# Score vectors as extra columns of the layer matrices, bias rows added inside the linear attention, and kept rows and result moved tile by tile

## The chip, the core and the metric

The kernel runs on one core of one Trainium2 chip. The metric is the device time of one execution in microseconds (us). The engines named below are TensorE (PE, with its weight loads as PEld), VectorE (DVE), ScalarE (ACT), GpSimd (POOL) and SyncE (SP, which here only issues transfers and waits).

## What is computed

Two layers of a graph transformer over 3125 nodes with 256 features. What matters here is the second layer's front and end, and the four graph attention projections. For the graph attention layers g0 (layer 0), g1, g2, g3 (layer 1), the projection is

```python
h = (x @ W).reshape(n, heads, out_ch)
al_s = jnp.einsum('nhc,hc->nh', h, a_src)      # one score per node and head
al_d = jnp.einsum('nhc,hc->nh', h, a_dst)
...
out = softmax over incoming edges(al_s[src] + al_d[dst]) applied to h[src];  return out + b
```

g0 has 4 heads of 64 features and 256 inputs, g1 4 heads of 128 and 256 inputs, g2 4 heads of 128 and 512 inputs, g3 one head of 256 and 512 inputs. Layer 1 begins with a linear attention whose output, plus a bias `b_out`, is added to X; the three graph attentions follow, then a small MLP (M1, M2, M3 with last bias `mb3`) whose output is added to the same X, and a gated feed-forward network whose output is added to X and is the result.

## The kernel before, in words

Rows are cut into T = 25 tiles of R = 125 rows; loops take U = 5 tiles an iteration. X lives in SBUF as [125, 25, 256]. The program is a row of stages (`Stage`): each has its own buffers and semaphores, and ends with a barrier of all engines. Within a stage the engines run freely against semaphores. `tile_dma` (L63) cuts each transfer into two, partitions 0 to 111 (L65) and 112 to 124 (L66). `wait_apart` is a wait followed by an increment of a tick semaphore.

**The projection stage** `stage_gat_project` (L686, stages g0p, g1p, g2p, g3p). SP loads the matrix `w`, the two score vectors `att` (broadcast to all partitions) and the bias `bt`. DVE folds each 128-row chunk of W with the score vectors into `wa` (L780, L782), so that the scores are x @ wa. Then for each tile PE makes h into the PSUM tile `psh` (L751) and the 2 x heads scores into `psa` (L753); DVE adds the bias and writes HX (L791) and writes the negated scores to AL (L794). An f32 matmul shows as two records in the trace; KC is 2 (g0, g1) or 4 (g2, g3) chunks. In g0p and g1p POOL copies the tile's columns of XT to `xs`; in g2p and g3p the rows come from DRAM by SP into five buffers, PE turns them (L742) and ACT copies them to `xs` (L804). PE may run two tiles ahead of DVE: it waits for `h_free` and `al_free` of the tile two before.

**Around the linear attention.** `stage_linear_attention` (stage lina, then linb) makes a 256 x 256 matrix WEFF. Stage lo (`stage_rows_add`) adds XT @ WEFF to X tile by tile: POOL copies, PE multiplies (L672), DVE adds (L2093). Stage ar1 (`stage_add_row`) adds two bias rows to all of X on DVE. Stage sv (`stage_move_rows`) writes X to DRAM (`kept_rows`), because the graph attentions need the SBUF space. Then g1p follows.

**Around the third graph attention.** After g1, g2 and g3, stage ld1 reads `kept_rows` back into X, stage tn (`stage_turn`) reads g3's output rows and transposes them, and the MLP and gates follow. In the attention stages (g3a) SP loads one tile row of `lowered` (`nl`, 1.5 MB) for each tile of rows.

**The end.** `stage_last_ffn` adds five products per tile to X on DVE (L2183, L2186); stage st writes X to the output in one transfer (two parts).

Of the kernel before, what the change touches and what calls it, by code (L numbers as in the profile page):

```python
# [685 lines left out]
def stage_gat_project(nc, m, g, feed, KC, w, att_s, att_d, bias, AL, HX):  # L686

    H, F, HF = g.heads, g.feat, g.heads * g.feat
    from_rows = feed.shape[0] == N
    with Stage(nc, g.name + "p") as s:  # L690
        wt = s.sb("w", [P, KC, HF])
        att, prod = s.sb("att", [P, 2, HF]), s.sb("prod", [P, 2, HF])
        wa = s.sb("wa", [P, KC, 2 * H])
# [38 lines left out]
        def _(pe):  # L732
# [23 lines left out]
            pe.wait_ge(loaded, 64)  # L756
# [1623 lines left out]
```

## Time and profile before

| | value |
|---|---|
| median of 3 runs | 5582.71 us (5581.7 to 5585.99) |
| the profiled execution | 5571.72 us, its span 5570.1 us |
| PE busy | 4657.3 us, 84% of the span |
| DVE busy | 3214.9 us, 58% |
| ACT busy | 2853.6 us, 51% |
| POOL busy | 1528.0 us, 27% |
| mean granted TensorE clock | 0.897 of full |
| moved by DMA | 479.79 MB, mean 86 GB/s |

The shares are averages over several dozen stages. What a change in one stage is worth must be read from that stage's own stretch: which engine is waited for there, and in the stretches in which nothing but a transfer runs, how long that transfer lasts.

### The profile page before, as it was taken

How to read it: one execution, taken by the hardware profiler on the slowest of the kernel's cores; microseconds unless marked ns; L12 is line 12 of the kernel's file. 1: busy time of each engine (PE TensorE's matmuls, PEld its weight loads, DVE VectorE, ACT ScalarE, POOL GpSimd, SP SyncE). 2: the span in 40 equal slices, each digit the busy share in tenths (PEclk: the TensorE clock that was granted, in tenths of full speed). 3: DMA queues.
4: the chain of work that ended last, by engine and by line, in shares of the span. 5: the costliest groups of instructions: out<-in, count | busy, mean ns of one | idle time of the engine just before them, and what ended most of it. 6: DMA issues, size and time to landing. Idle time of an engine off the chain costs nothing. (4 is left out here: it accounts for less than half of the span.)

```text
span 5570.1 us, 94226 instructions
## 1 busy us (share of the span) xinstructions
PE 4657.3 (84%) x34254; PEld 4166.0 (75%) x34254; DVE 3214.9 (58%) x2815; ACT 2853.6 (51%) x3886; POOL 1528.0 (27%) x1308
## 2 busy tenths in 40 slices
PE   1554779999998469938699999979999998897698
PEld 1453457999998369934399999948999997786454
DVE  4894213887887401134388888717888882552222
ACT  0662133777776024313078877716778773443222
POOL 3001000221222310040146666602666661010100
PEclk9776788999999589969899999989999999998767
DMA  2672011333332245520144434323443442553000
GB/s 47 110 141 39 3 69 45 91 95 87 101 92 57 84 154 182 185 81 16 47 105 102 107 98 105 82 62 94 106 103 98 108 101 58 141 129 79 7 11 23
DMA packets 212766, 479.79 MB, mean 86 GB/s; under 512 B 117787, under 2 KB 158886, under 8 KB 189417
## 3 DMA queue, kind: packets, MB, share of 16 engines
q1 hardware_dynamic: 178982, 436.39, 30.1%
q0 software_dynamic: 24720, 30.26, 2.6%
q10 hardware_dynamic: 8736, 8.39, 0.5%
q8 instruction: 252, 4.13, 0.3%
q14 instruction: 76, 0.62, 0.0%
HBM read 391.43 MB, written 83.35 MB: 85 GB/s over the span
## 5 line engine op out<-in xcount | busy, mean ns | idle before, releaser
L1105 PE MATMUL g2a_pso<-HX,g2a_wt 125*125 125x129 f32 x5000 | 602.7, 274 | 8.0 <-DVEq L952 4.7
L1105 PE MATMUL g1a_pso<-HX,g1a_wt 125*125 125x129 f32 x5000 | 603.1, 274 | 4.5 <-ACT g1a_wt L989 3.3
L1105 PE MATMUL g0a_pso<-HX,g0a_wt 125*125 125x65 f32 x5000 | 595.1, 274 | 4.8 <-ACT g0a_wt L989 3.3
L1105 PEld LDWEIGHTS g0a_pso<-HX,g0a_wt 125*125 125x125 f32 x5000 | 585.2, 193 | 5.3 <-ACT g0a_wt L989 3.4
L1105 PEld LDWEIGHTS g2a_pso<-HX,g2a_wt 125*125 125x125 f32 x5000 | 576.3, 189 | 8.4 <-DVEq L952 4.9
L1105 PEld LDWEIGHTS g1a_pso<-HX,g1a_wt 125*125 125x125 f32 x5000 | 576.8, 189 | 5.0 <-ACT g1a_wt L989 3.5
L989 ACT ACTIVATE g0a_wt<-g0a_pst 125x1000 f32<-125x1000 f32 (+1 forms) x300 | 312.0, 1040 | 199.6 <-PE g0a_pst L1092 199.6
L922 DVE SCALAR_TENSOR_TENSOR g0a_x<-g0a_als,g0a_cd,HX 125x3125 f32<-125x3125 f32 x100 | 347.4, 3474 | 110.9 <-PE g0a_pst L1092 101.7
L922 DVE SCALAR_TENSOR_TENSOR g2a_x<-g2a_als,g2a_cd,g2a_as 125x3125 f32<-125x3125 f32 x100 | 358.7, 3587 | 81.3 <-PE g2a_pst L1092 71.3
L922 DVE SCALAR_TENSOR_TENSOR g1a_x<-g1a_als,g1a_cd,g1a_as 125x3125 f32<-125x3125 f32 x100 | 358.1, 3581 | 81.4 <-PE g1a_pst L1092 71.5
L989 ACT ACTIVATE g2a_wt<-g2a_pst 125x1000 f32<-125x1000 f32 (+1 forms) x300 | 312.2, 1041 | 170.3 <-PE g2a_pst L1092 170.3
L989 ACT ACTIVATE g1a_wt<-g1a_pst 125x1000 f32<-125x1000 f32 (+1 forms) x300 | 312.2, 1041 | 169.5 <-PE g1a_pst L1092 169.5
L927 DVE CUSTOM_DVE_ANT_0 g2a_x<-g2a_x,g2a_nl 125x3125 f32<-125x3125 f32 x100 | 344.7, 3447 | 20.0 <-issue 14.3
L927 DVE CUSTOM_DVE_ANT_0 g1a_x<-g1a_x,g1a_nl 125x3125 f32<-125x3125 f32 x100 | 344.8, 3448 | 19.6 <-issue 13.9
L927 DVE CUSTOM_DVE_ANT_0 g0a_x<-g0a_x,g0a_nl 125x3125 f32<-125x3125 f32 x100 | 341.5, 3415 | 19.6 <-issue 13.9
L1092 PE MATMUL g0a_pst<-C,g0a_x 125*125 125x125 f32 x2500 | 347.1, 284 | 3.6 <-ACT g0a_x L981 3.6
L981 ACT ACTIVATE g2a_x<-g2a_x,g2a_top 125x1000 f32<-125x1000 f32 (+1 forms) x300 | 346.6, 1156 | 3.8 <-DVEq L929 3.8
L981 ACT ACTIVATE g0a_x<-g0a_x,g0a_top 125x1000 f32<-125x1000 f32 (+1 forms) x300 | 346.6, 1156 | 1.9 <-DVEq L929 1.9
L981 ACT ACTIVATE g1a_x<-g1a_x,g1a_top 125x1000 f32<-125x1000 f32 (+1 forms) x300 | 346.6, 1156 | 1.6 <-DVEq L929 1.6
L1092 PE MATMUL g1a_pst<-C,g1a_x 125*125 125x125 f32 x2500 | 322.9, 273 | 3.6 <-ACT g1a_x L981 3.6
L1092 PE MATMUL g2a_pst<-C,g2a_x 125*125 125x125 f32 x2500 | 323.0, 273 | 2.2 <-ACT g2a_x L981 2.2
L1092 PEld LDWEIGHTS g0a_pst<-C,g0a_x 125*125 125x125 f32 x2500 | 306.5, 194 | 3.8 <-ACT g0a_x L981 3.8
(428 smaller groups left out, 8429.4 us busy)
## 6 DMA issues: line engine op xcount, KB each, us to landing
g0a_nl<-lowered SPq DMA_DIRECT2D x50, 1367.2 KB
g1a_nl<-lowered SPq DMA_DIRECT2D x50, 1367.2 KB
g2a_nl<-lowered SPq DMA_DIRECT2D x50, 1367.2 KB
moe_wa<-in_L_ffn_W SPq DMA_DIRECT2D x56, 1024.0 KB, 4.9
lowered<-counts_nl SPq DMA_DIRECT2D x25, 1367.2 KB
g3a_nl<-lowered SPq DMA_DIRECT2D x25, 1367.2 KB
g0a_nl<-lowered SPq DMA_DIRECT2D x50, 158.7 KB
g1a_nl<-lowered SPq DMA_DIRECT2D x50, 158.7 KB
```

The source lines that it names most:

```text
L922: nc.vector.scalar_tensor_tensor(out=x[:, b, :], in0=als[:, h, :], scalar=cd[:, h:h + 1, ds(t, 1)].rearrange("p a b -> p (a b)"), in1=as2[ ...
L927: nc.vector.tensor_tensor_reduce(out=x[:, b, :], in0=x[:, b, :], in1=nl[:, (q + k // HG) % 2, :], scale=1.0, scalar=3e38, op0=ALU.add, op1 ...
L981: nc.scalar.activation(x[:, b, c0:c1], x[:, b, c0:c1], ACT.Exp, bias=top[:, b:b + 1], scale=-1.0).then_inc(exped, 1)
L989: nc.scalar.activation(wt[:, side, 0:n * R].rearrange("p (b n) -> p b n", b=banks), pst[0:R, 3 * side:3 * side + banks, 0:per * R], ACT.Co ...
L1092: last = nc.tensor.transpose(pst[0:R, 3 * side + j // per, col:col + R], x[:, ring(q, k), (a0 + j) * R:(a0 + j + 1) * R], m.ident[0:R, 0:R])
L1105: last = nc.tensor.matmul(pso[0:R, unit(q, 0, k) % 2, 0:F + 1], wt[:, side, j * R:(j + 1) * R], HX[:, a, q * HG + k % HG, :], start=(a == ...
```

## The change

**Projection.** Each matrix is stored in SBUF with the score vectors' products as extra columns behind it: `wt` is [P, KC, PARTS, WP + SC], where PARTS is 2 for the 512-wide layers (g1, g2) and 1 otherwise. DVE's fold writes straight into those columns. PE's matmuls make 264 (g0), 260 (g1, g2, in two halves, one PSUM bank each) or 258 (g3) columns, and the separate score matmuls are gone. DVE's two instructions a tile stay, and read the same banks. W is loaded by KC transfers, not one.

**Bias rows.** They are loaded in the linear attention stage and added to X there, one tile after each tile's `scale`; stage ar1 is gone.

**Kept rows.** Stage lo's SP stores each tile as soon as DVE has added it, and stage sv is gone; the end of g1p waits for the stores. The reload is issued by g3p's SP after its last row tile, stage ld1 is gone, and the end of stage tn waits for it.

**Result.** In the last stage DVE signals each finished tile and SP stores it; stage st is gone.

```diff
-def stage_gat_project(nc, m, g, feed, KC, w, att_s, att_d, bias, AL, HX):
+def stage_gat_project(nc, m, g, feed, KC, w, att_s, att_d, bias, AL, HX, kept=None, ahead=None):
 
     H, F, HF = g.heads, g.feat, g.heads * g.feat
+    PARTS = max(HF // 256, 1)
+    HP, WP = H // PARTS, HF // PARTS
+    SC = 2 * H // PARTS
     from_rows = feed.shape[0] == N
     with Stage(nc, g.name + "p") as s:
-        wt = s.sb("w", [P, KC, HF])
+        if kept is not None:
+            s.sems.append(kept)
+        wt = s.sb("w", [P, KC, PARTS, WP + SC])
         att, prod = s.sb("att", [P, 2, HF]), s.sb("prod", [P, 2, HF])
-        wa = s.sb("wa", [P, KC, 2 * H])
         bt = s.sb("bt", [R, HF])
         xs = s.sb("xs", [P, U, KC, R])
-        psh, psa = s.ps("psh", 3), s.ps("psa", 3)
+        ps = s.ps("ps", 3 * PARTS)
...
-            sp.dma_start(wt[:], w.rearrange("(c p) n -> p c n", p=P)).then_inc(loaded, 16)
+            for c in range(KC):
+                sp.dma_start(wt[:, c, :, 0:WP], w[c * P:(c + 1) * P].rearrange("p (x n) -> p x n", x=PARTS)).then_inc(loaded, 16)
...
+            if ahead is not None:
+                tile_dma(sp, *ahead)
+            if kept is not None:
+                sp.wait_ge(kept, 32 * T)
...
-                for c in range(KC):
-                    nc.tensor.matmul(psh[0:R, RING3[k], 0:HF], xs[:, k, c, :], wt[:, c, :], start=(c == 0), stop=(c == KC - 1))
-                for c in range(KC):
-                    last = nc.tensor.matmul(scores(k), xs[:, k, c, :], wa[:, c, :], start=(c == 0), stop=(c == KC - 1))
+                for x in range(PARTS):
+                    for c in range(KC):
+                        last = nc.tensor.matmul(banks(k)[:, x, 0:WP + SC], xs[:, k, c, :], wt[:, c, x, :], start=(c == 0), stop=(c == KC - 1))
                 last.then_inc(full, 1)
...
-                last = nc.vector.tensor_reduce(wa[:, c, :], prod[:].rearrange("p j (h f) -> p (j h) f", h=H), AX_X, ALU.add)
+                last = nc.vector.tensor_reduce(wt[:, c, :, WP:WP + SC], prod[:].rearrange("p j (h f) -> p (j h) f", h=H), AX_X, ALU.add)
...
-                    nc.vector.tensor_tensor(HX[:, ds(t, 1), :, 0:F].rearrange("p o h f -> p (o h) f"),
-                                            psh[0:R, RING3[k], 0:HF].rearrange("p (h f) -> p h f", h=H),
-                                            bt[:].rearrange("p (h f) -> p h f", h=H), ALU.add).then_inc(h_free, 1)
-                    nc.vector.tensor_scalar(AL[:, 0:2 * H, ds(t, 1)], scores(k).unsqueeze(2), -1.0, None, ALU.mult).then_inc(al_free, 1)
+                    nc.vector.tensor_tensor(HX[:, ds(t, 1), :, 0:F].rearrange("p o (x h) f -> p (o x) h f", x=PARTS),
+                                            banks(k)[:, :, 0:WP].rearrange("p x (h f) -> p x h f", h=HP),
+                                            bt[:].rearrange("p (x h f) -> p x h f", x=PARTS, h=HP), ALU.add).then_inc(h_free, 1)
+                    nc.vector.tensor_scalar(AL[:, 0:2 * H, ds(t, 1)].rearrange("p (x n) o -> p x (n o)", x=PARTS), banks(k)[:, :, WP:WP + SC],
+                                            -1.0, None, ALU.mult).then_inc(al_free, 1)
...
+                for j, v in enumerate(vectors):
+                    sp.dma_start(rows[:, j, :], v.partition_broadcast(R)).then_inc(rows_in, 16)
...
                 variance(0)
+                dve.wait_ge(rows_in, 32)
+                nc.vector.tensor_tensor(rows[:, 0, :], rows[:, 0, :], rows[:, 1, :], ALU.add)
                 for t in range(T):
                     if t + 1 < T:
                         variance(t + 1)
                     scale(t)
+                    nc.vector.tensor_tensor(X[:, t, :], X[:, t, :], rows[:, 0, :], ALU.add)
...
+            if KEEP is not None:
+                with sp.Fori(0, T // U) as i:
+                    for k in range(U):
+                        t = i * U + k
+                        wait_apart(sp, s.tick, rp.free[0], t + 3)
+                        tile_dma(sp, KEEP[:, ds(t, 1)].rearrange("p o d -> p (o d)"), cols(X[:, ds(t, 1), :]), kept)
...
+            with sp.Fori(0, T // U) as j:
+                for k in range(U):
+                    t = j * U + k
+                    wait_apart(sp, s.tick, rows_done, t + 1)
+                    tile_dma(sp, OUT[ds(t * R, R)], cols(X[:, ds(t, 1), :]), stored)
+            sp.wait_ge(stored, 32 * T)
...
+                    nc.vector.drain().then_inc(rows_done, 1)
...
-                stage_linear_attention(nc, m, a, XT, WEFF)
-                stage_rows_add(nc, m, "lo", [(XT, 2, WEFF)], X)
-                stage_add_row(nc, "ar1", [a["L1_gnn_mb3"], a["L1_mix_b_out"]], X)
-                stage_move_rows(nc, "sv", m.XS, X)
-                stage_gat_project(nc, m, g1, XT, 2, a["L1_gnn_W1"], a["L1_gnn_a_src1"], a["L1_gnn_a_dst1"], a["L1_gnn_b1"], AL, rows_of(g1))
-        for g, n in ((g1, 1), (g2, 2), (g3, 3)):
-            if n > 1:
-                stage_gat_project(nc, m, g, m.Y, 4, a[f"L1_gnn_W{n}"], a[f"L1_gnn_a_src{n}"], a[f"L1_gnn_a_dst{n}"], a[f"L1_gnn_b{n}"], AL, rows_of(g))
-            graph_attention(nc, m, g, AL, rows_of(g), m.Y[:, 0:g.heads * g.feat])
-
-
+                stage_linear_attention(nc, m, a, XT, WEFF, [a["L1_gnn_mb3"], a["L1_mix_b_out"]], X)
+                kept = nc.alloc_semaphore("rows_kept")
+                stage_rows_add(nc, m, "lo", [(XT, 2, WEFF)], X, m.XS, kept)
+                stage_gat_project(nc, m, g1, XT, 2, a["L1_gnn_W1"], a["L1_gnn_a_src1"], a["L1_gnn_a_dst1"], a["L1_gnn_b1"], AL, rows_of(g1), kept)
...
-            stage_move_rows(nc, "ld1", X, m.XS)
+            x_back = nc.alloc_semaphore("x_back")
+            stage_gat_project(nc, m, g3, m.Y, 4, a["L1_gnn_W3"], a["L1_gnn_a_src3"], a["L1_gnn_a_dst3"], a["L1_gnn_b3"], AL, rows_of(g3), None, (X, m.XS, x_back))
...
-            stage_last_ffn(nc, m, a, XT, GATE, X)
-            stage_move_rows(nc, "st", out.rearrange("(t p) d -> p t d", p=R), X)
+            stage_last_ffn(nc, m, a, XT, GATE, X, out)
```

What PE runs in two tiles of g2p before (a row with x4 is four matmuls, L742 the transposes, psh the product, psa the scores):

```order
L751 MATMUL g2p_psh<-g2p_w,g2p_xs 125x512 x4
L753 MATMUL g2p_psa<-g2p_wa,g2p_xs 125x8 x4
L742 MATMUL g2p_pst<-C,g2p_rows 128x125 x4
L747 REGISTER_ALU
L751 MATMUL g2p_psh<-g2p_w,g2p_xs 125x512 x4
L753 MATMUL g2p_psa<-g2p_wa,g2p_xs 125x8 x4
```

And the same place of the changed kernel:

```order
L761 MATMUL g2p_ps<-g2p_w,g2p_xs 125x260 x8
L751 MATMUL g2p_pst<-C,g2p_rows 128x125 x4
L756 REGISTER_ALU
L761 MATMUL g2p_ps<-g2p_w,g2p_xs 125x260 x8
L751 MATMUL g2p_pst<-C,g2p_rows 128x125 x4
```

Four wide and four narrow matmuls have become eight of 260 columns. The next piece is SP's program between the linear attention and the projection g1p, before: two stages of their own for the bias rows and the kept rows.

```order
L1189 DMA ar_v<-in_L_gnn_mb 125x256
L1189 DMA ar_v<-in_L_mix_b_out 125x256
L57 UNCONDITIONAL_BRANCH
L2203 UNCONDITIONAL_BRANCH
L65 DMA kept_rows<-X 112x6400
L66 DMA kept_rows<-X 13x6400
L57 UNCONDITIONAL_BRANCH
L707 UNCONDITIONAL_BRANCH
L709 DMA g1p_w<-in_L_gnn_W 128x2x512
```

After the change, the end of the loop in stage lo (the last of its five tiles) and what follows it:

```order
L71 REGISTER_ALU
L65 ISA
L65 DMA kept_rows<-X 112x256
L66 ISA
L66 DMA kept_rows<-X 13x256
L2099 REGISTER_ALU
L2099 COMPARE_AND_BRANCH
L57 UNCONDITIONAL_BRANCH
L711 UNCONDITIONAL_BRANCH
L714 DMA g1p_w<-in_L_gnn_W 128x2x256 x2
```

Two transfers have become fifty, issued in the loop of stage lo, and the branch to g1p stands right behind that loop. The third place is the end of g3p on SP in the changed kernel, where the reload now stands ahead of the attention's first `nl` tiles:

```order
L65 DMA g3p_rows<-attended 112x512
L66 ISA
L66 DMA g3p_rows<-attended 13x512
L721 REGISTER_ALU
L721 COMPARE_AND_BRANCH
L65 DMA X<-kept_rows 112x6400
L66 DMA X<-kept_rows 13x6400
L57 UNCONDITIONAL_BRANCH
L909 UNCONDITIONAL_BRANCH
L65 DMA g3a_nl<-lowered 112x3125
L66 DMA g3a_nl<-lowered 13x3125
```

Before, those two reload rows stood behind the whole attention stage, ahead of `tn_rows`.

## Rows read from the trace of the kernel before

**Rows 1.** Busy time by stretch: stage lo, stage sv. us, PE, PEld, DVE, ACT, POOL, PEclk, DMA share, GB/s

```profile
2650.00:2674.00 24.00, 22.72 (x100) 16.51 (x98) 10.54 (x25) 0.00 (x0) 8.90 (x23) 1.00 0.00 0
2692.60:2706.10 13.50, 0.00 (x0) 0.00 (x0) 0.00 (x0) 0.00 (x0) 0.00 (x0) 0.50 0.73 237
```

**Rows 2.** Timeline, g3p: start, us, engine, line, out<-in, count, idle before and releaser

```profile
4670.06 1.59 PEld L751 LDWEIGHTS g3p_psh<-g3p_w,g3p_xs 128*125 128x125 f32 x8
4670.16 1.89 PE L751 MATMUL g3p_psh<-g3p_w,g3p_xs 128*125 128x256 f32 x8
...
4671.89 0.93 PE L753 MATMUL g3p_psa<-g3p_wa,g3p_xs 128*125 128x2 f32 x8
...
4672.68 0.62 PE L742 MATMUL g3p_pst<-C,g3p_rows 125*128 125x125 f32 x4
...
4673.14 0.38 PE L751 MATMUL g3p_psh<-g3p_w,g3p_xs 128*125 128x256 f32 x1
```

**Rows 3.** Timeline, g2p, PE in one tile

```profile
3669.01 3.60 PE L751 MATMUL g2p_psh<-g2p_w,g2p_xs 128*125 128x512 f32 x8
...
3672.44 0.94 PE L753 MATMUL g2p_psa<-g2p_wa,g2p_xs 128*125 128x8 f32 x8
```

**Rows 4.** Timeline, g1p, PE at the start of two tiles

```profile
2725.61 1.96 PE L751 MATMUL g1p_psh<-g1p_w,g1p_xs 128*125 128x512 f32 x4
...
2727.77 0.67 PE L751 MATMUL g1p_psh<-g1p_w,g1p_xs 128*125 128x512 f32 x1
```

**Rows 5.** Timeline, g0p, PE at two tiles, DVE at one

```profile
492.72 1.11 PE L751 MATMUL g0p_psh<-g0p_w,g0p_xs 128*125 128x256 f32 x4
...
494.02 1.11 PE L751 MATMUL g0p_psh<-g0p_w,g0p_xs 128*125 128x256 f32 x4
...
494.41 0.42 DVE L791 TENSOR_TENSOR HX<-g0p_psh,g0p_bt 125x256 f32 x1 [0.79 <-PE g0p_psa L753]
...
494.75 0.16 DVE L794 TENSOR_SCALAR AL<-g0p_psa 125x8 f32 x1
```

**Rows 6.** Timeline, stage lo, DVE two tiles apart

```profile
2663.76 0.42 DVE L2093 TENSOR_TENSOR X<-X,lo_ps 125x256 f32 x1 [0.53 <-PE lo_ps L672]
...
2665.58 0.42 DVE L2093 TENSOR_TENSOR X<-X,lo_ps 125x256 f32 x1 [0.54 <-PE lo_ps L672]
```

**Rows 7.** Timeline, stage tn, SP's issues for two tiles

```profile
5131.65 0.33 SPq L65 DMA_DIRECT2D tn_rows<-attended  x1
...
5132.84 0.32 SPq L65 DMA_DIRECT2D tn_rows<-attended  x1
```

**Rows 8.** Timeline, first add of lo, first issues of ar1 and g1p

```profile
2650.98 0.42 DVE L2093 TENSOR_TENSOR X<-X,lo_ps 125x256 f32 x1 [19.21 <-PE lo_ps L672]
...
2674.00 0.33 SPq L1189 DMA_DIRECT2D ar_v<-in_L_gnn_mb  x1
...
2706.12 0.40 SPq L709 DMA_DIRECT2D g1p_w<-in_L_gnn_W  x1
```

**Rows 9.** Timeline, stage lina, DVE at the start of a tile

```profile
2621.62 1.22 DVE L1987 TENSOR_REDUCE lina_var<-lina_sq 125x16 f32<-125x1024 f32 x1 [1.99 <-ACT lina_sq L2015]
```

**Rows 10.** Timeline, end of g3a, starts of ld1 and tn

```profile
5106.03 0.52 POOL L66 DMA_DIRECT2D attended<-g3a_y  x1
5109.35 0.31 SPq L65 DMA_DIRECT2D X<-kept_rows  x1
...
5127.14 0.32 SPq L65 DMA_DIRECT2D tn_rows<-attended  x1
```

**Rows 11.** Timeline, start of g3a: first nl issue, first use

```profile
4739.54 0.33 SPq L65 DMA_DIRECT2D g3a_nl<-lowered  x1
...
4751.40 3.42 DVE L927 CUSTOM_DVE_ANT_0 g3a_x<-g3a_x,g3a_nl 125x3125 f32<-125x3125 f32 x1 [0.24 <-issue]
```

**Rows 12.** Timeline, last add of the program and the result's store

```profile
5553.57 0.48 DVE L2186 SCALAR_TENSOR_TENSOR X<-ffn_psy,GATE,X 125x256 f32 x1 [0.38 <-PE ffn_psy L2157]
5555.43 0.35 SPq L65 DMA_DIRECT2D out<-X  x1
```

More of the change, by code:

```diff
@@ L702, in stage_gat_project, with banks @@
         block = s.block()
-        def scores(k):
-            return psa[0:R, RING3[k], 0:2 * H]
+        def banks(k):
+            return ps[0:R, RING3[k] * PARTS:(RING3[k] + 1) * PARTS, :]
         @block.sync
         def _(sp):
-            sp.dma_start(wt[:], w.rearrange("(c p) n -> p c n", p=P)).then_inc(loaded, 16)
+            for c in range(KC):
+                sp.dma_start(wt[:, c, :, 0:WP], w[c * P:(c + 1) * P].rearrange("p (x n) -> p x n", x=PARTS)).then_inc(loaded, 16)
             for j, a in enumerate((att_s, att_d)):
@@ L749, in multiply @@
                 pe.wait_ge(al_free, t + 1)
[L750 to L753 removed]
+                for x in range(PARTS):
+                    for c in range(KC):
+                        last = nc.tensor.matmul(banks(k)[:, x, 0:WP + SC], xs[:, k, c, :], wt[:, c, x, :], start=(c == 0), stop=(c == KC - 1))
                 last.then_inc(full, 1)
[L756 removed]
+            pe.wait_ge(loaded, 16 * (KC + 3))
             if not from_rows:
@@ L775, in _ @@
         def _(dve):
-            dve.wait_ge(loaded, 64)
+            dve.wait_ge(loaded, 16 * (KC + 3))
             for c in range(KC):
                 for j in range(2):
-                    nc.vector.tensor_tensor(prod[:, j, :], wt[:, c, :], att[:, j, :], ALU.mult)
+                    nc.vector.tensor_tensor(prod[:, j, :].rearrange("p (x n) -> p x n", x=PARTS), wt[:, c, :, 0:WP],
+                                            att[:, j, :].rearrange("p (x n) -> p x n", x=PARTS), ALU.mult)
                 nc.vector.drain()
-                last = nc.vector.tensor_reduce(wa[:, c, :], prod[:].rearrange("p j (h f) -> p (j h) f", h=H), AX_X, ALU.add)
+                last = nc.vector.tensor_reduce(wt[:, c, :, WP:WP + SC], prod[:].rearrange("p j (h f) -> p (j h) f", h=H), AX_X, ALU.add)
                 if c < KC - 1:
@@ L1139, in graph_attention, with stage_turn @@
     stage_gat_attend(nc, m, g, AL, HX, OUT, X, spare)
-def stage_turn(nc, m, name, ROWS, KC, outT):
+def stage_turn(nc, m, name, ROWS, KC, outT, before):
     with Stage(nc, name) as s:
+        s.sems.append(before)
         rows = s.sb("rows", [R, U, KC * P])
@@ L1157, in _ @@
                     tile_dma(sp, rows[:, k, :], ROWS[ds((i * U + k + U) * R, R)], rows_in[k])
+            sp.wait_ge(before, 32)
         @block.tensor
@@ L1918, in _, with stage_linear_attention @@
             sums.root(act)
-def stage_linear_attention(nc, m, a, xT, WEFF):
+def stage_linear_attention(nc, m, a, xT, WEFF, vectors, X):
     HEADS, DH = 8, 64
@@ L1936, in stage_linear_attention @@
             ps, psd = s.ps("ps", 6), s.ps("psd", 1)
+            rows, rows_in = s.sb("rows", [R, 2, D]), s.sem("rows_in")
             loaded, centred, full, free, v_free, squared, var_ready, std_ready, k_ready, v_ready, dotted = [
@@ L2059, in _, with stage_rows_add @@
                 nc.scalar.activation(WEFF, psw[:, :, 0:D], ACT.Copy)
-def stage_rows_add(nc, m, name, parts, X):
+def stage_rows_add(nc, m, name, parts, X, KEEP=None, kept=None):
     with Stage(nc, name) as s:
@@ L2094, in _, with stage_last_ffn @@
             rp.read(dve, add)
-def stage_last_ffn(nc, m, a, xT, GATE, X):
+def stage_last_ffn(nc, m, a, xT, GATE, X, OUT):
     E = 4
@@ L2110, in stage_last_ffn @@
         loaded, h_full, h_ready, y_full, y_free = [s.sem(n) for n in ("loaded", "h_full", "h_ready", "y_full", "y_free")]
+        rows_done, stored = s.sem("rows_done"), s.sem("stored")
         block = s.block()
@@ L2187, in _ @@
                         nc.vector.drain()
+                    nc.vector.drain().then_inc(rows_done, 1)
 class Machine:
     pass
-def stage_move_rows(nc, name, dst, src):
-    with Stage(nc, name) as s:
-        moved = s.sem("moved")
-        block = s.block()
-        @block.sync
-        def _(sp):
-            tile_dma(sp, dst, src, moved)
-            sp.wait_ge(moved, 32)
 def build(nc, a, out):
```

6 lines of the change are left out of this document (5 added, 1 removed).

## The prediction

> **What bounds the kernel now.** The page says that PE is busy most of the span, but the change leaves the three long attention stages alone, so I read the stretches that it touches, by busy time first. Two kinds show. In stage sv, and likewise in ar1, ld1 and st, one thing runs and the rest waits: in sv nothing is busy but the DMA, at 237 GB/s [rows 1]. There the stage's length is the price. In the projections PE is the engine waited for, and the timeline gives its beat as differences between starts. In g3p the eight records of h take 1.73 us (4670.16 to 4671.89), the eight of the scores 0.79 us, the four transposes 0.46 us: 2.98 us a tile [rows 2]. A score record has 2 columns and still costs 0.1 us. In g2p the wide part takes 3.43 us [rows 3], and its scores and transposes what they take in g3p. A tile takes 2.16 us in g1p [rows 4] and 1.30 us in g0p [rows 5].
>
> **Projections, PE.** A 256-column record costs 1.73 / 8 = 0.216 us [rows 2], a 512-column one 3.43 / 8 = 0.429 us [rows 3]; the slope is 0.00083 us a column, and cutting 512 in two costs nearly nothing.
> - g3p: 1.73 + 8 x 2 columns x 0.00083 = 1.74 us, in place of 1.73 + 0.79. It saves 0.78 us a tile, 19.5 us in 25.
> - g2p: sixteen records of 260: 2 x 1.73 + 16 x 4 x 0.00083 = 3.51 us, in place of 3.43 + 0.79 = 4.22. 0.71 a tile, 17.8 us.
> - g1p: eight records of 260: 1.73 + 0.03 = 1.76 us, in place of 2.16 [rows 4]. 0.40 a tile, 10 us.
> - g0p: four of 264: 0.87 + 0.02 = 0.89 us in place of 1.30 [rows 5]; but here the next limit comes up. PE waits for DVE's work on the tile two before. Stage lo is this pattern already: four records of 256 and one DVE add. Its DVE starts lie 1.82 us apart over two tiles [rows 6], which is 0.87 for PE, 0.42 for DVE and so 0.53 for the two handovers. In g0p DVE has two instructions, 0.34 + 0.16 = 0.50 us from the first's start to the second's end [rows 5]. The cycle is 0.89 + 0.53 + 0.50 = 1.92 us for two tiles, 0.96 each. 0.34 a tile, 8.5 us, not the 10.3 of PE alone.
>
> In the others that cycle stays below PE's beat: for g1p 1.76 + 0.53 + at most twice 0.50 for twice the columns is 3.3 for two tiles, against 3.5. With a 2.2 us beat g3p's rows (250 KB a tile) need 114 GB/s, and sv shows that 237 is possible [rows 1]; SP needs 1.19 us for a tile's two issues [rows 7]. Both are hidden. W now comes in one transfer more (g0p, g1p) or three more (g2p, g3p), at 0.40 us an issue [rows 8], ahead of the last load that DVE's fold waits for. Full cost: 0.4 and 1.2 us; in g2p and g3p I take 0.8, as megabytes already queue on those transfers and part of the later issue hides behind them. The fold itself has the same instructions and sizes. Sum: 8.1 + 9.6 + 17.0 + 18.7 = 53.4 us. The bounds are 48 (g0p gains half, loads in full) and 57.
>
> The Trainium skill speaks against the halving (TensorE: Matmul & The Clock Gate, Back-to-back issue gap): in a stream of weight load and matmul pairs the spacing is set by both, so twice as many loads could bind. The row shows eight loads taking 1.59 us under 1.73 us of matmuls [rows 2], so they still hide, though narrowly. By the page's 2.5 ns per matmul at full clock, my estimate is a cost of 0.75 us for the 300 extra records of g1p and g2p.
>
> **Bias rows and kept rows.** From the first issue of ar1 at 2674.00 to that of g1p at 2706.12 are 32.1 us [rows 8], and both stages go. What comes back is twofold. DVE adds a 125 x 256 tile in stage lina, at most 0.42 us by lo's add [rows 6], where it waits 1.99 us in each tile [rows 9]: free but for the last tiles, 0.3 us. Without that cover it would be 10 us. And SP must issue fifty stores inside lo. Its pace in tn, where nothing else holds it, is 1.19 us a tile [rows 7], slower than lo's 0.91 [rows 6]. The first add ends at 2651.4 [rows 8]; 25 tiles of stores end at 2681.1, and with 0.7 us for the barrier g1p starts near 2681.8. That is 7.8 us after 2674.00. Net 32.1 - 7.8 - 0.3 = 24.0 us. The stores' addresses are computed on both sides, tn's on one only. No row shows that price: it lies between nothing (24.0) and as much again as a computed address adds now. That I bound by tn's 1.19 less two plain issues of 0.40 [rows 8], 0.39 us a tile, 9.8 us (14.2). SP's program has the same number of rows a tile, so I take nothing. If SP kept lo's pace it would be 31.8. The wait for `kept` stands at the end of g1p, over 50 us later.
>
> **Reload.** ld1 is 5109.35 to 5127.14, 17.8 us [rows 10]. Its 3.1 MB now follow the last row tile of g3p, some 5.5 tiles or 12 us before that stage ends, and at 237 GB/s they need 13.2 us. What remains is in front of g3a's first `nl` tile, which was issued at 4739.54 and used at 4751.40, 11.9 us later [rows 11]; 1.5 MB need 6.6 us. So 5 us of slack take up a rest of 1 or 2 us; I charge 1.0. Net 16.8 us. If none of the reload ran under g3p it would arrive 13.2 us late, less the 5 of slack: net 9.6.
>
> **Result.** The last add ends at 5554.05, the store starts at 5555.43 [rows 12], and the span ends at 5570.1. Now only the last tile is stored after the add. g3a ends with such a store: its last issue begins at 5106.03 and the next stage at 5109.35 [rows 10], 3.3 us with barrier. With a handover and the first issue ahead (0.8 us) the end falls near 5554.05 + 0.8 + 3.3 = 5558.2. That saves 11.9 us. DVE's second drain in each tile falls where it waits 0.38 us for PE [rows 12]; uncovered, at 0.1 us, it would be 2.5.
>
> **Sum.** 53.4 + 24.0 + 16.8 + 11.9 = 106.1 us. The profiled execution took 5571.72 us and would take 5465.6. The median of the runs is 11 us above it, so the same saving gives 5582.71 - 106.1 = 5476.6 us.
>
> **Rivals.**
> - *Forecast*, 5466 to 5486: chance 0.66.
> - *SP's stores are slower*: computed addresses on both sides cost another 0.39 us a tile, g1p starts 9.8 us later, 5486. For it: nothing in the trace has both sides computed. Against: equal program rows. 0.11.
> - *The reload is in the attention's way*: `nl` comes late at g3a's start, up to 7 us more, 5484. For it: the queue is full there. Against: the slack [rows 11]. 0.10.
> - *The stores follow lo's pace, or drains and loads cost nothing*: 7.8 us better, 5469. 0.07. Against it stands [rows 7].
> - *The moves come back elsewhere*: the stages go but their transfers end the next stage just as late, so that the 52.7 us of moves are lost and only the projections gain, 5529. Against it: DMA is idle in lo and moves nothing [rows 1]. 0.01.
> - *PE's clock falls, slower than before*: the clock shows 0.50, 1.2 GHz, where PE idles in sv, and 1.00, 2.4 GHz, in lo [rows 1]. If the new projections ran at 1.2 GHz, records would take twice as long: 1.8 us a tile in g0p, 3.5 in g1p, 7.9 in g2p, 4.4 in g3p, in place of 1.30, 2.16, 4.68 and 2.98. That is +163 us for the four, where I have -53, and with the moves' -53 the kernel would be 110 us slower, 5693. It decides when about half of the projections' tiles run at 1.2 GHz. Against it: lo has just the small waits for DVE that g0p would get, and runs at 1.00. The Trainium skill describes this mechanism (same page, A second HAM failure mode: psum-queue depth-cycling): cycling through PSUM banks with small idles lets the clock swing. Lo's row shows no such swing. 0.03.
> - *It does not do what it says* (the score matmuls cost nothing on the path): against it stand the starts of the rows 0.79 us apart; what is left is within 0.2%. 0.02.
>
> **The numbers.** Faster by over 0.2% (11 us; about what a measurement of this kernel can tell from no change): 0.66 + 0.11 + 0.10 + 0.07 + 0.01 = 0.95. Same 0.02, slower 0.03. The range takes in the slow stores and the late reload, not both in full with all the rest: 5463 to 5494.
>
> **What would show it.** No matmul into a score tile, and starts 2.2 us apart in g3p, 3.97 in g2p, 1.76 in g1p, 0.96 in g0p. 1.3 in g0p would show that another limit holds there. g1p's first load some 24 us nearer to lina's end; SP's stores in lo 1.19 us a tile apart. tn's first load 3.3 us behind g3a's last store, and `nl`'s first use 12 to 13 us behind its issue. The span's end 4 us behind the last add. I am wrong if SP's pace, the reload or the clock differ, in that order.

## The result, and the profile after

The changed kernel took 5481.06 us (median of 4 runs, 5472.41 to 5489.65) against 5582.2 us of the kernel before beside it: ratio 0.9823, 95% interval 0.98 to 0.9846. The medians differ by 101.1 us, where 106.1 were forecast. A second set of five runs gave 0.9821 (0.9807 to 0.9836). The profiled execution took 5489.65 us, its span 5488.0, only 82 us under that of before. So I compare stretch by stretch, each measured from one stage's first issue to the next's.

| stretch | before, us | after, us | difference |
|---|---|---|---|
| counts to g0p (untouched) | 402.1 | 414.5 | +12.4 |
| g0p | 77.3 | 69.6 | -7.7 |
| g0a (untouched) | 893.8 | 901.7 | +7.9 |
| lina | 126.5 | 126.8 | +0.3 |
| linb to g1p's first load | 73.6 | 50.9 | -22.7 |
| g1p | 70.9 | 63.4 | -7.5 |
| g2p | 141.6 | 124.3 | -17.3 |
| g3p | 92.8 | 74.1 | -18.7 |
| g3a to tn | 387.6 | 369.8 | -17.8 |
| ffn's first load to the span's end | 252.3 | 242.4 | -9.9 |

The eight touched stretches sum to -101.3 us, which is what the medians say. The two untouched ones, +20 us, come up again in experiment 12.

The timeline after, g3p, then two tiles of g2p, of g1p and of g0p (start, us, engine, line, out<-in, count, idle before and releaser):

```profile
4652.26 0.43 DVE L800 TENSOR_TENSOR HX<-g3p_ps,g3p_bt 125x256 f32 x1 [1.69 <-PE g3p_ps L761]
4652.27 1.91 PE L761 MATMUL g3p_ps<-g3p_w,g3p_xs 128*125 128x258 f32 x8
4654.43 0.43 DVE L800 TENSOR_TENSOR HX<-g3p_ps,g3p_bt 125x256 f32 x1 [1.68 <-PE g3p_ps L761]
...
3699.87 0.69 DVE L800 TENSOR_TENSOR HX<-g2p_ps,g2p_bt 125x512 f32 x1 [3.16 <-PE g2p_ps L761]
3703.81 0.69 DVE L800 TENSOR_TENSOR HX<-g2p_ps,g2p_bt 125x512 f32 x1 [3.17 <-PE g2p_ps L761]
...
2736.25 0.69 DVE L800 TENSOR_TENSOR HX<-g1p_ps,g1p_bt 125x512 f32 x1 [0.99 <-PE g1p_ps L761]
2738.00 0.69 DVE L800 TENSOR_TENSOR HX<-g1p_ps,g1p_bt 125x512 f32 x1 [0.98 <-PE g1p_ps L761]
...
515.89 0.42 DVE L800 TENSOR_TENSOR HX<-g0p_ps,g0p_bt 125x256 f32 x1 [0.68 <-PE g0p_ps L761]
516.23 0.17 DVE L803 TENSOR_SCALAR AL<-g0p_ps 125x8 f32 x1
516.51 0.74 PEld L761 LDWEIGHTS g0p_ps<-g0p_w,g0p_xs 128*125 128x125 f32 x4 [0.40 <-POOL g0p_xs L738]
516.78 0.42 DVE L800 TENSOR_TENSOR HX<-g0p_ps,g0p_bt 125x256 f32 x1 [0.39 <-PE g0p_ps L761]
517.92 0.42 DVE L800 TENSOR_TENSOR HX<-g0p_ps,g0p_bt 125x256 f32 x1 [0.63 <-PE g0p_ps L761]
```

A tile now takes 2.17 us in g3p, 3.94 in g2p, 1.75 in g1p. In g0p two tiles take 2.03 us: the weight load at 516.51 starts 0.11 us after DVE's second instruction ends (516.40). POOL is named as releaser, but its copy had long been done; the wait is for `al_free`.

The first tiles of three projections are slower in this trace. From the first add to the second are 2.97 us in g1p (2.16 before) and 2.57 in g3p, and g0p's first two tiles take 1.78 and 1.75 us. The granted clock there is 0.50 (1.2 GHz), behind it 1.00. The start of g1p's tiles (columns as in [rows 1]):

```profile
2714.00:2717.80 3.80, 3.80 (x10) 2.96 (x9) 0.77 (x2) 0.00 (x0) 0.40 (x1) 0.50 0.00 0
```

Stage lo and g1p's start after (answers to [rows 8]):

```profile
2664.87 0.42 DVE L2117 TENSOR_TENSOR X<-X,lo_ps 125x256 f32 x1 [19.37 <-PE lo_ps L672]
2665.55 0.37 SPq L65 DMA_DIRECT2D kept_rows<-X  x1
...
2687.68 0.42 DVE L2117 TENSOR_TENSOR X<-X,lo_ps 125x256 f32 x1 [0.54 <-PE lo_ps L672]
...
2694.23 0.32 SPq L65 DMA_DIRECT2D kept_rows<-X  x1
...
2695.40 0.32 SPq L65 DMA_DIRECT2D kept_rows<-X  x1
2695.91 0.32 SPq L66 DMA_DIRECT2D kept_rows<-X  x1
2697.14 0.68 SPq L714 DMA_DIRECT2D g1p_w<-in_L_gnn_W  x1
```

DVE is done at 2688.1. SP's last issue begins 7.8 us later (1.17 us a tile here, 1.24 from the first store to the last), and g1p waits for it. In lina DVE's idle time at the start of a tile fell from 1.99 [rows 9] to 1.43 us: the new add lies in it.

g3p's end and g3a (answers to [rows 10, 11]), and the program's end (answers to [rows 12]):

```profile
4671.12 0.35 SPq L65 DMA_DIRECT2D X<-kept_rows  x1
...
4685.86 0.32 SPq L65 DMA_DIRECT2D g3a_nl<-lowered  x1
...
4697.80 3.42 DVE L937 CUSTOM_DVE_ANT_0 g3a_x<-g3a_x,g3a_nl 125x3125 f32<-125x3125 f32 x1 [0.24 <-issue]
...
5052.61 0.52 POOL L66 DMA_DIRECT2D attended<-g3a_y  x1
5055.70 0.31 SPq L65 DMA_DIRECT2D tn_rows<-attended  x1
...
5484.35 0.48 DVE L2217 SCALAR_TENSOR_TENSOR X<-ffn_psy,GATE,X 125x256 f32 x1 [0.38 <-PE ffn_psy L2188]
5485.20 0.32 SPq L65 DMA_DIRECT2D out<-X  x1
```

The first `nl` is used 11.94 us after its issue (11.86 before), with the same 0.24 us of idle time that no wait explains: the reload costs nothing there. The span ends at 5488.0, 3.2 us behind the last add.

### The profile page after: what moved, and what is told of

Same layout as the page of the kernel before. It is cut to its first block and busy times, and to the rows that moved or that the text cites. A ratio compares the mean times of both kernels' runs of the same rounds, so it can differ in the third digit from the quotient of the medians.

```text
span 5488.0 us, 94007 instructions
## 1 busy us (share of the span) xinstructions
PE 4612.3 (84%) x33954; PEld 4166.1 (76%) x33954; DVE 3211.0 (59%) x2839; ACT 2853.2 (52%) x3886; POOL 1531.7 (28%) x1308
```

## The experiments

Kernels 1, 2, 3 and 6 ran four times each, 11 and 12 five times. Kernels 4, 5, 7, 8, 9 and 10 ran once each, beside one run of the kernel before (5458.44, 5467.63, 5444.18 and 5467.75 us for 5568.81; 5447.07 and 5474.3 for 5576.9). As untouched stretches alone differ by up to 22 us between traces, only stretches are compared for these six.

**1 and 2. The parts apart.** The first kernel is the kernel before with the changed `stage_gat_project` alone; the second is the changed kernel with the old projection, whose core is this:

```diff
-                for x in range(PARTS):
-                    for c in range(KC):
-                        last = nc.tensor.matmul(banks(k)[:, x, 0:WP + SC], xs[:, k, c, :], wt[:, c, x, :], ...)
+                for c in range(KC):
+                    nc.tensor.matmul(psh[0:R, RING3[k], 0:HF], xs[:, k, c, :], wt[:, c, :], ...)
+                for c in range(KC):
+                    last = nc.tensor.matmul(scores(k), xs[:, k, c, :], wa[:, c, :], ...)
```

> Only the projection's part of the change (score columns, W in KC transfers) on the kernel before; bias rows, kept rows, reload and result stay in stages of their own. The theory of the prediction (a term for each part, and the terms add): the four projections give back 7.7 + 7.5 + 17.3 + 18.7 = 51.2 us as in the changed kernel's trace, tile periods about 1.03, 1.75, 3.94 and 2.17 us, nothing else moves, ratio near 0.991. Rival (the narrow matmuls were hidden, and the gain of the changed kernel comes from the moved transfers alone): the ratio stays within 0.2% of 1. Rival (the parts help each other, for instance the transfers gain only because the projections are shorter or the other way): the projections' stretches differ by several us from the changed kernel's.

> The complement: the changed kernel with the old projection (512-wide matmuls, separate scores, W in one transfer), but with bias rows, kept rows, reload and result moved. If the terms add: linb to g1p 22.7 us shorter, ld1's 17.8 us gone, the last stretch 9.9 us shorter, 50 us in all, ratio near 0.991; the four projections as before. The reload is the place where they could fail to add: here g3p's tiles take 2.98 us, so 5.5 tiles are 16.4 us of cover in place of 12, and the attention's first nl tile should be used 11.9 us after its issue all the same. If instead the shorter projection were what exposes the reload, nl's first use would come earlier here than in the changed kernel, where it is 11.94 us behind its issue.

Measured: scores alone 5526.57 us, ratio 0.9898 (0.9881 to 0.9914); moves alone 5529.11 us, 0.9899 (0.9882 to 0.9916). The product is 0.9798, just below the changed kernel's interval (0.98 to 0.9846), which comes from other runs. Kernel 6 below, the changed kernel but for one drain, was measured beside these two and has 0.9797. Scores alone: g0p -9.1, g1p -7.4, g2p -16.5, g3p -18.7 us, sum 51.7; linb to g1p 73.8, g3a to tn 386.6 as before. Moves alone: linb to g1p 50.6, g3a to tn 369.6, last stretch 238.3, and the four projections within 0.9 us of before; first `nl` used 11.85 us behind its issue. The parts add; that the narrow matmuls or the transfers were hidden is refuted.

**3. Kept rows behind g1p's loads.**

```diff
-                stage_rows_add(nc, m, "lo", [(XT, 2, WEFF)], X, m.XS, kept)
-                stage_gat_project(..., rows_of(g1), kept)
+                stage_rows_add(nc, m, "lo", [(XT, 2, WEFF)], X)
+                stage_gat_project(..., rows_of(g1), kept, (m.XS, X, kept))
```

> Changed kernel, but X is written to kept_rows in one transfer (two issues) behind g1p's loads, with stage lo free of stores. My theory that SP's pace of 1.2 us a tile sets lo's length: lo ends at PE's pace, first load of g1p 9 us nearer (linb to g1p 41.8 in place of 50.9 us), g1p itself as long as now (63.4 us) because the 3.1 MB stand behind the loads in the queue and need about 13 us of its 46 us of tiles; kernel 9 us faster than the changed one. Rival: the transfer shares the DMA engines with W's load, which ends later; g1p up to 5 us longer, gain of 4. Rival: lo is bound by something else (the clock at its start, POOL) and the stretch stays near 50 us.

Measured: 5468.24 us, ratio 0.9796 (0.9779 to 0.9813). Linb to g1p fell from 50.9 to 42.5 us; g1p took 62.9, its load 9.9 us where it had 8.9. That is no sign of a collision, as kernel 4, without this transfer, has a load of 9.9 us too. A 3.1 MB transfer for which nobody waits until the stage ends, 60 us later, cost nothing that shows, although 325 GB/s move while the fold runs, and the fold keeps its 5.26 us:

```profile
2685.50:2690.70 5.20, 0.00 (x0) 0.00 (x0) 4.96 (x6) 0.00 (x0) 0.00 (x0) 0.50 0.86 325
```

The stretch of 42.5 us is 0.7 longer than I expected. Lo's second add comes 1.69 us behind its first, 0.88 in the kernel before, and the granted clock there is 0.50, where it was 1.00.

**4. One store a tile.** The changed kernel, with the store not cut at partition 112.

```diff
-                        tile_dma(sp, KEEP[:, ds(t, 1)]..., cols(X[:, ds(t, 1), :]), kept)
+                        sp.dma_start(KEEP[:, ds(t, 1)]..., cols(X[:, ds(t, 1), :])).then_inc(kept, 16)
```

> Changed kernel, but each tile of kept_rows is stored in lo by one transfer of 125 partitions, not by 112 and 13: 25 issues in place of 50. If SP's work per issue sets lo's length (0.51 and 0.66 us between the starts of a tile's two issues), a tile costs SP about 0.6 us, less than PE's 0.91, and the stretch from linb's first load to g1p's falls from 50.9 to about 43 us, near the 42.5 that it has with no stores in lo at all. Rival: it is the bytes, or how an uneven number of partitions spreads over the DMA engines, and the issue is held back; then the stretch stays near 50 us and the stores' spacing near 1.2 us.

Measured: linb to g1p 44.0 us. In its timeline the first of the rows below holds nine stores in 8.17 us, in step with DVE's adds, and g1p's load is issued 2.5 us behind the start of the last add, where the changed kernel has 9.5. So it was the issue work of SP. Half the issues, though over fewer DMA engines, let the stores follow the adds.

```profile
2660.41 8.17 SPq L2103 DMA_DIRECT2D kept_rows<-X  x9
...
2667.03 0.42 DVE L2117 TENSOR_TENSOR X<-X,lo_ps 125x256 f32 x1 [0.54 <-PE lo_ps L672]
2669.51 0.68 SPq L714 DMA_DIRECT2D g1p_w<-in_L_gnn_W  x1
```

**5. Five banks in g0p.**

```diff
-        ps = s.ps("ps", 3 * PARTS)
+        DEPTH = 5 if PARTS == 1 else 3       # bank k, not RING3[k], where 5
+        ps = s.ps("ps", DEPTH * PARTS)
...
-            dve.sem_inc(al_free, 2)          # and act.sem_inc(h_free, ...)
+            dve.sem_inc(al_free, 4 if DEPTH == 5 else 2)
```

> Changed kernel, but in g0p and g3p (one bank a tile) PE has five banks in turn and may run four tiles ahead of DVE, not two. The prediction said that in g0p the cycle PE, handover, DVE, handover over two tiles sets the pace; in the trace it is 1.02 us a tile. If so, PE's own beat (0.89 us and a little) takes its place: 0.9 us a tile, g0p's tiles from 27.7 (26.4 to 27.7 in the traces so far) to 24 to 25 us. If another limit holds (POOL's copy, SP, the program rows between the matmuls) they stay at 26.4 or more. In g3p PE's 2.17 us a tile are longer than the cycle and nothing should change: 55.4 us.

Measured, from PE's first product matmul in the stage to its last: g0p 24.7 us, from 26.4 to 27.7 in the traces with three banks; g3p 55.7, as in the others that load W alike (55.3 to 55.8). Two neighbouring tiles of g0p in its timeline:

```profile
505.87 0.42 DVE L802 TENSOR_TENSOR HX<-g0p_ps,g0p_bt 125x256 f32 x1 [0.38 <-PE g0p_ps L763]
...
506.76 0.42 DVE L802 TENSOR_TENSOR HX<-g0p_ps,g0p_bt 125x256 f32 x1 [0.39 <-PE g0p_ps L763]
```

0.89 us apart is PE's own beat. In the changed kernel's timeline above the same starts lie 0.89 and 1.14 us apart in turn: the cycle with DVE was the limit.

**6. One drain less in the last stage.**

```diff
-                        nc.vector.drain()
-                    nc.vector.drain().then_inc(rows_done, 1)
+                        last = nc.vector.drain()
+                    last.then_inc(rows_done, 1)
```

> Changed kernel, with the tile's last drain in the last stage carrying the signal for the store, so that DVE has five drains a tile again and not six. In the changed kernel the time from the stage's first load to the end of the last add is 239.2 us, before it was 236.25. Theory A: the sixth drain is not covered as I had said, and costs 0.08 us or so a tile; the time falls back by 2 us, to about 237.2 (one us of the rest lies ahead of the first add). Theory B: the stores' traffic or SP's issues slow the adds, and the drain is covered: it stays at 239.2.

Measured: 5470.46 us, ratio 0.9797 (0.978 to 0.9813), and 234.8 us from first load to the end of the last add, 2.4 less than theory A wanted, so neither theory fits. From first to last add it is 201.5 us; kernel 3, with six drains, has 201.8, and kernel 1, with five drains and no stores, 201.4. Neither drain nor stores show, beyond 0.4 us. What goes with the 205.7 us of the changed kernel's trace (204.9 in its second) is a lower clock. The last stage from first to last add: the kernel before, changed, scores only, store under g1p, one drain (columns as in [rows 1]):

```profile
5349.80:5553.60 203.80, 199.77 (x536) 111.42 (x535) 58.42 (x125) 45.74 (x88) 0.00 (x0) 0.73 0.00 0
```

```profile
5278.60:5484.30 205.70, 201.57 (x536) 112.52 (x535) 58.44 (x124) 45.74 (x88) 0.00 (x0) 0.72 0.05 15
```

```profile
5307.70:5509.10 201.40, 197.19 (x536) 109.48 (x535) 58.45 (x124) 45.74 (x88) 0.00 (x0) 0.74 0.00 0
```

```profile
5258.60:5460.40 201.80, 197.22 (x536) 109.74 (x535) 58.47 (x124) 45.74 (x88) 0.00 (x0) 0.74 0.05 15
```

```profile
5253.90:5455.40 201.50, 197.17 (x536) 109.54 (x535) 58.42 (x124) 45.81 (x88) 0.00 (x0) 0.74 0.05 15
```

DVE's work is the same, PE's busy time follows the clock, and the length follows PE. The clock's means lie between its levels, 0.50 (1.2 GHz) and 1.00 (2.4 GHz). In the changed kernel it is 1.00 while PE runs the hidden layers of five tiles without a gap. It is still 1.00 when PE comes to the adds (5277.8), where it waits for DVE in each product, falls in the course of them, and is 1.00 again with the next hidden layers:

```profile
5262.00:5274.60 12.60, 12.60 (x49) 8.45 (x48) 0.00 (x0) 6.90 (x14) 0.00 (x0) 1.00 0.00 0
5274.60:5278.60 4.00, 3.31 (x13) 1.54 (x12) 0.00 (x0) 2.97 (x6) 0.00 (x0) 1.00 0.02 4
5282.60:5286.60 4.00, 3.77 (x10) 1.43 (x8) 2.25 (x5) 0.00 (x0) 0.00 (x0) 0.76 0.11 32
5286.60:5305.60 19.00, 19.00 (x40) 10.60 (x40) 7.07 (x15) 0.94 (x2) 0.00 (x0) 0.51 0.09 27
5305.10:5325.10 20.00, 19.23 (x72) 11.92 (x71) 0.91 (x2) 10.91 (x21) 0.00 (x0) 1.00 0.00 0
```

**7. How W is loaded.**

```diff
-            for c in range(KC):
-                sp.dma_start(wt[:, c, :, 0:WP], w[c * P:(c + 1) * P]...).then_inc(loaded, 16)
+            for x in range(PARTS):
+                sp.dma_start(wt[:, :, x, 0:WP], w[:, x * WP:(x + 1) * WP]...).then_inc(loaded, 16)
```

> Changed kernel, but W comes in one transfer for each part of 256 columns (one in g0p and g3p, two in g1p and g2p) instead of one for each chunk of rows (2, 4, 2, 4). From the first issue to DVE's first fold instruction the trace of the changed kernel has 5.3, 9.1 (g3p), 8.9 (g1p) and 12.0 us (g2p), before 5.4, 8.7, 7.6 and 10.5. Theory A, number of issues: g1p stays at 8.9 or more (same number), g2p falls by 0.8 to 1.2 us, g3p by 0.4 to 1.2. Theory B, the piece of a row that one descriptor carries (1 KB in g1p and g2p now, 2 KB before): g1p and g2p stay 1.3 to 1.5 us above before, g3p and g0p stay as they are.

Measured, first issue to first fold: g2p 10.4 us (12.0, and 11.4 to 12.3 in the others), g3p 7.9 (9.1), g1p 8.4 (8.9, and 7.9 to 9.9 in the others), g0p 5.3 (5.3). The number of transfers explains g2p and g3p, and theory B falls for g2p. The gain goes with SP's time: W takes 2.57 us of issues in g2p in the changed kernel (3623.88 to 3626.45) and 0.99 here, 1.82 and 0.45 in g3p. In g1p nothing is decided within its scatter.

**8. The reload doubled.**

```diff
+                    tile_dma(sp, m.X9, m.XS, ahead[2])     # DRAM to DRAM, 3.1 MB
                 tile_dma(sp, *ahead)
```

> Changed kernel, with the reload's cost doubled or more: ahead of the reload g3p's SP also copies kept_rows to a spare array in DRAM (3.1 MB read and written once more, result unused). In the changed kernel the reload cost nothing that the trace shows: g3a's first nl tile is used 11.94 us after its issue, as before. By the sum (12 us of g3p's end, 5 us of slack at g3a's start, 237 GB/s) two such moves need 26.4 us, so that the first use slips by about 26.4 - 12 - 5 = 9 us, and g3a to tn is 369.8 + 9. If the reads and writes run beside each other on many engines, or nl has a way past them, it slips by under 3 us; if the copy runs at half rate because DRAM is on both ends, by 20 us or more.

```profile
4664.01 0.32 SPq L65 DMA_DIRECT2D g3a_nl<-lowered  x1
...
4684.15 3.42 DVE L939 CUSTOM_DVE_ANT_0 g3a_x<-g3a_x,g3a_nl 125x3125 f32<-125x3125 f32 x1 [8.53 <-DMA g3a_nl<-lowered]
```

The first use came 20.1 us behind the issue, 8.2 later, and now DVE waits for the DMA, 8.53 us. Forecast were 9. But the single reload of the changed kernel had used nothing of the slack at g3a's start. It is issued 14.7 us ahead of `nl` (4671.12 to 4685.86), not 12, and its transfer is over before that:

```profile
4671.10:4684.70 13.60, 13.11 (x71) 10.97 (x69) 3.19 (x13) 2.94 (x5) 0.00 (x0) 1.00 1.02 255
4684.70:4685.80 1.10, 0.00 (x0) 0.00 (x0) 0.25 (x2) 0.00 (x0) 0.00 (x0) 1.00 0.01 0
```

With 26.4 us for the two moves and 14.7 of cover, a slip of 8.2 leaves 3.5 us of slack, an estimate from the 237 GB/s of [rows 1]. G3a to tn took 375.1 us, 5.3 to 7.0 more than in the kernels with one reload and the fold unchanged (368.2 to 369.8), so the stage takes a part of the delay back.

**9. The fold chunk by chunk.**

```diff
-            for c in range(KC): ... .then_inc(loaded, 16)
             for j, a in enumerate((att_s, att_d)):
-                sp.dma_start(...).then_inc(loaded, 16)
+                sp.dma_start(...).then_inc(att_in, 16)
+            for c in range(KC): ... .then_inc(chunk_in[c], 16)
...
-            dve.wait_ge(loaded, 16 * (KC + 3))
+            dve.wait_ge(att_in, 32)
             for c in range(KC):
+                dve.wait_ge(chunk_in[c], 16)
```

> Changed kernel, but the score vectors are loaded first, each chunk of W has a semaphore of its own, and DVE folds chunk c as soon as it is there (the bias is waited for behind the fold). Now the fold waits for all of W, both vectors and the bias: 12.0 us in g2p, 9.1 in g3p, 8.9 in g1p, 5.3 in g0p, and then takes 11.8, 7.5, 5.7 and 3.6 us. Theory (the load's length is bytes, 1.75 MB in g2p at some 200 GB/s, and the last of them are what the fold waits for): with 1 of 1.75 MB off the wait the first fold starts about 4 us earlier in g2p, 2 in g3p and g1p, under 1 in g0p, and each fold stays as long as it is, since a chunk lands in about 1.3 us and takes 2.9 us to fold; all four together about 9 us. Rival: the score vectors' broadcast, every partition reading the same rows, is what takes long (8 us in g2p); then nothing is gained.

Measured: g0p's stretch 67.2 us (69.6); from linb's first load to ffn's 2581.9 in place of 2599.4 us, 17.5 less, twice what I had expected. From the first fold instruction to PE's first product the stages took as long as before (11.8, 7.5, 5.6, 3.5 us). In g2p the score vectors are issued first, and the fold starts 5.25 us later, not 12.0:

```profile
3597.45 0.35 SPq L715 DMA_DIRECT2D g2p_att<-in_L_gnn_a_src  x1
...
3602.70 1.29 DVE L789 TENSOR_TENSOR g2p_prod<-g2p_w,g2p_att 128x512 f32<-128x512 f32 x2 [15.98 <-DMA g2p_w<-in_L_gnn_W]
```

Of these 6.8 us, 3.1 are issues. In the changed kernel the last transfer that the fold waits for, the bias, is issued 3.95 us behind the first (3623.88 to 3627.83), here W's first chunk 0.87 us behind (3597.45 to 3598.32). From that issue to the fold are 8.1 and 4.4 us: the 3.7 us less are what my sum had for the bytes. The issues it had left out, which is why the gain was twice the sum.

**10. Bias rows in lo.**

```diff
-                    nc.vector.tensor_tensor(X[:, t, :], X[:, t, :], rows[:, 0, :], ALU.add)   # lina
...
+            for j, v in enumerate(vectors):                                                       # lo's SP
+                sp.dma_start(rows[:, j, :], v.partition_broadcast(R)).then_inc(rows_in, 16)
...
                 xt = cols(X[:, ds(t, 1), :])
+                nc.vector.tensor_tensor(xt, xt, rows[:, 0, :], ALU.add)                       # lo
+                nc.vector.drain()
```

> Changed kernel, but the bias rows are added to each tile in stage lo, ahead of the product's add and with a drain between, and not in the linear attention. Lo's cycle over two tiles (PE 0.87, handovers 0.53, DVE 0.42 us) becomes 0.5 longer, 1.17 us a tile in place of 0.91. Theory: SP's stores at 1.19 us a tile set lo's length in the changed kernel, so that this costs nothing or up to 1 us: linb to g1p 51 to 52 us, and the linear attention's stretch falls by 0.3 us at most (126.8 to 126.5). Rival: PE and DVE set lo's length: 25 x 0.26 = 6.5 us more, 57 us.

Measured: linb to g1p 56.8 us, 5.9 more, which looks like the rival. The timeline says otherwise:

```profile
2642.86 0.33 SPq L2095 DMA_DIRECT2D lo_rows<-in_L_gnn_mb  x1
...
2647.57 0.43 DVE L2115 TENSOR_TENSOR lo_rows<-lo_rows 125x256 f32<-125x256 f32 x1 [21.98 <-DMA lo_rows<-in_L_mix_b_out]
2648.17 2.04 PE L672 MATMUL lo_ps<-WEFF,lo_xs 128*125 128x256 f32 x4 [6.62 <-DVEq L2116]
```

DVE waits for the bias rows before it opens the PSUM slots, and PE's first matmul waits 6.62 us for that. From the first store (2651.5) to the last (2681.9) it is 30.4 us; in the changed kernel, 2665.55 to 2695.91, also 30.4. DVE's longer cycle was hidden under SP's pace; the load at the start was not, a cost that my sum for this edit had left out.

**11 and 12. Together, and the changed kernel again.** Kernel 11 joins 3, 5, 6 and 9.

> What gained alone, in one kernel: kept_rows in one transfer behind g1p's loads, five banks in g0p and g3p, the fold chunk by chunk with the score vectors first, one drain less in the last stage (which gained nothing that the trace shows). If the gains add: from linb's first load to the last stage's first load the changed kernel has 2599.4 us in its trace, the transfer under g1p gave 2592.8, the fold by chunk 2581.9; together 2575. g0p's stretch 64.7 us (69.6 in the changed kernel, 67.2 and 66.6 with one of the two). Kernel 27 us faster than the changed one, some 5453 us, ratio to the kernel before 0.977. If the moved store collides with the loads, now that the fold starts on the first chunk, g1p's stretch shows it: 57.7 us with the fold by chunk alone.

> The changed kernel once more, unchanged, to learn how far the stretches that the change does not touch differ between executions. In its first trace the stretch from counts to g0p was 414.5 us (402.1 before), g0a's 901.7 (893.8 before), the last stage's first to last add 205.7 (203.8 before). If these belong to the changed program, they return: 414, 902, 206. If they are the execution's own, they lie anywhere among what the other runs had (402 to 415, 880 to 902, 201 to 206), and the median lies near 5582 - 106 = 5476 us, ratio 0.981 to 0.983.

Measured: together 5438.2 us, ratio 0.9771 (0.9757 to 0.9785); the changed kernel beside it 5465.4, 0.9821 (0.9807 to 0.9836): 27.2 us less, as the parts' sum had it. Linb to ffn 2571.9, g0p 64.9, g1p 58.5. With the fold by chunk alone g1p took 57.7; the 0.8 between them lie within what its load differs by between traces, so a collision with the store is neither shown nor excluded. The changed kernel again: counts 402.1, g0a 901.8, first to last add 204.9. So the 12.4 us in counts were that execution's own; the fourteen traces have 402.1 to 414.5. In g0a two traces of the changed kernel agree at 902, but kernel 6, which differs from it only in the last stage, has 879.8. The whole stage in the changed kernel, before, and kernel 6 (columns as in [rows 1]):

```profile
930.20:1831.90 901.70, 874.95 (x7650) 869.52 (x7650) 721.20 (x411) 668.50 (x742) 197.95 (x176) 0.95 0.34 88
```

```profile
924.90:1818.70 893.80, 867.10 (x7650) 862.32 (x7650) 721.09 (x411) 668.28 (x742) 201.02 (x176) 0.96 0.35 89
```

```profile
926.70:1806.50 879.80, 852.90 (x7650) 847.95 (x7650) 721.20 (x411) 668.65 (x742) 207.57 (x176) 0.98 0.35 90
```

Granted clock 0.95, 0.96, 0.98, with the same work. Whether that level is the execution's own or comes with the program is not decided, as the only kernel traced twice gave the same both times; the mean clock of its five runs here lies between 0.896 and 0.902, so part of it does change between executions.

## Why the prediction was right

The time (5476.6 for 5481.06) and the mechanisms held. The terms missed by -2.2 us (projections), -1.6 (bias and kept rows), +1.0 (reload) and -2.0 (result). For the single profiled execution the forecast was 5465.6 and the time 5489.65; 20 of these 24 us are the two untouched stretches. That the medians came out nearer has a share of luck, as nothing in the sum dealt with such differences between executions.

- **Projections, PE.** 2.17, 3.94, 1.75 us a tile where 2.20, 3.97, 1.76 were forecast. The rule of the Trainium skill that spoke against the halving (TensorE: Matmul & The Clock Gate, Back-to-back issue gap) would have made tiles longer. By its 2.5 ns the eight extra records of a g2p tile are 0.02 us, my estimate. The tile came out 0.03 us below the sum, so a cost as small as that can be neither seen nor excluded; that twice as many weight loads bind is refuted.
- **g0p's cycle.** "0.96 each" is 1.02: PE and handovers take 1.52 us in the cycle, not 1.42. Experiment 5 shows that the cycle, not another limit, set it.
- **"0.40 us an issue", W's transfers.** The mis-sized step. In the changed kernel's trace the load phase grew by 1.3 us in g1p and 1.5 in g2p where I charged 0.4 and 0.8; two issues of W start 0.7 us apart (1.33 us for two, from 2697.14). In g3p it grew by 0.4, less than the 0.8. Experiment 7 shows the cost in g2p to be SP's issues: two fewer take 1.6 us off them and 1.6 off the load phase. The four terms together gave 51.2 us for 53.4, g1p alone 7.5 for 9.6: 0.9 us of that are the load, 1.2 its first tile at the lower clock, which no term had.
- **Kept rows.** "7.8 us after 2674.00" is 9.25: from lo's first add to the next stage's first issue are 32.27 us (2664.87 to 2697.14), before 23.02 [rows 8]. The pace was 1.24 us a tile, not 1.19. With lina's 0.3, as forecast, the net is 22.4 us for 24.0. The rival with slower stores (1.58 us) fell, as did the one in which they follow lo's 0.91. Experiment 3 shows 8.4 of the 9.25 us to be SP's issues, and experiment 4 that half as many save 6.9. The rest goes with the start of lo, which is granted 0.50 in every kernel with the moved rows (second add 1.69 or 1.72 us behind the first) and 1.00 in the two without (0.88); why was not tried.
- **Reload.** The 1.0 us charged for it did not appear: 17.8 for 16.8. The step that was off is the cover, 14.7 us and not 12, so that nothing of the reload remains in front of `nl`. Experiment 8 shows slack of about 3.5 us, not 5.
- **Result.** The end behind the last add came out at 3.2 us, not 4. But the stage before that add was 2.9 us longer, so that the stretch gave 9.9 for 11.9. The extra time goes with a lower clock, in both traces of this kernel, and not with the drain, which was covered as forecast (experiment 6): kernels 2, 3, 6 and 11, with the same stores, have the stretch at 237.9 to 238.3, 14 less than before, and the changed kernel again, at 0.72, has 241.4. Why the clock differs is open.
- **Clock.** The rival of a lower clock in the projections fell: but for the first tiles, the tile times are those of full clock. The swings that the Trainium skill describes (TensorE: Matmul & The Clock Gate, A second HAM failure mode: psum-queue depth-cycling) do show, in the last stage, which cycles through three banks in waits for DVE and is granted 0.72 to 0.74, but before the change as well. In g0p, with three banks and waits for DVE too, the changed kernel is granted 1.00 from 502.6 us on, so such waits alone do not bring them on:

```profile
502.60:525.00 22.40, 21.95 (x88) 14.41 (x86) 11.11 (x45) 0.00 (x0) 6.92 (x18) 1.00 0.00 0
```

## What to carry to other kernels

A transfer that only has to be done by some later time belongs where its issuing engine is idle, in few pieces: fifty issues inside a 23 us loop cost 8 us, two issues behind the next stage's loads cost nothing. When a load feeds a chain of work, give each piece its own semaphore and load first what every piece needs; that gave 17.5 us here, as much as hiding the whole reload. Count the issues ahead of the last transfer that is waited for, not only its bytes. When totals scatter by 10 us, compare untouched stretches first, and put the sum of the touched ones beside the medians.
